# Context attention in a two-layer decoder: probabilities first in the transpose queue, position angles and rope steps moved

## The reference, cut to what matters

```
q = rms_norm((x @ Wq.T).reshape(b, 128, 16, 128), q_norm_w)
kv_in = concatenate([context, x], axis=1)                 # 128 + 128 tokens
k = rms_norm((kv_in @ Wk.T).reshape(b, 256, 4, 128), k_norm_w)
v = (kv_in @ Wv.T).reshape(b, 256, 4, 128)
q, k = rope(q, positions), rope(k, all positions)         # x*cos + rotate_half(x)*sin
probs = softmax(q @ k.T / sqrt(128))                      # 16 query heads, 4 key/value heads
x = layernorm(x + (probs @ v) @ Wo.T)
```

## Time and profile before

| what | value |
|---|---|
| median of 3 runs | 3082.08 us (3080.01 to 3082.26) |
| profiled execution, its own time | 3079.49 us |
| its span, first to last instruction | 3077.7 us |
| context attention in it | some 465 to 1373 us |
| busy share of the whole span | PE 87%, DVE 64%, ACT 52%, POOL 43% |
| mean granted TensorE clock | 0.953 of full speed |

### The profile page before, as it was taken

How to read it: one execution, slowest core, us unless ns; L and a number is a source line. 1 busy time by engine, 2 the same in 40 slices (tenths; PEclk the granted TensorE clock), 3 DMA queues, 4 the chain that set the end, 5 groups by cost and what they waited for, 6 DMA issues and landing times. The chain is left out here.

```text
span 3077.7 us, 47741 instructions
## 1 busy us (share of the span) xinstructions
PE 2672.8 (87%) x16117; PEld 1504.0 (49%) x16380; DVE 1956.4 (64%) x3457; ACT 1604.5 (52%) x3757; POOL 1331.9 (43%) x1334
## 2 busy tenths in 40 slices
PE   6788895688888888857995899998989999999998
PEld 4676662344443444423443666665654444444443
DVE  5788986677777777747855788887563223332325
ACT  7999964555555555537434776776532212222111
POOL 4888977866656565603333311111142212222121
PEclk8999997899999999989997899999989999999999
DMA  4111105443334333433003000000012011111101
GB/s 159 41 53 46 44 27 144 98 79 69 76 75 78 72 76 75 77 89 116 1 1 110 22 22 14 14 18 19 15 67 77 31 63 63 60 64 34 63 30 67
DMA packets 287059, 181.05 MB, mean 59 GB/s; under 512 B 243585, under 2 KB 248065, under 8 KB 284706
## 3 DMA queue, kind: packets, MB, share of 16 engines
q1 hardware_dynamic: 286882, 178.74, 22.2%
...
## 5 line engine op out<-in xcount | busy, mean ns | idle before, releaser
L2065 POOL TENSOR_TENSOR s_state<-s_state,s_ct 128x512 f32<-128x512 f32 x256 | 326.6, 1298 | 81.8 <-DVE s_state L2240 79.4
L779 POOL TENSOR_TENSOR m_aTl<-m_prod,m_aTh 128x512 bf16<-128x512 f32 x88 | 101.7, 1155 | 583.9 <-ACT m_aTh L855 583.9
L2240 DVE TENSOR_TENSOR_SCAN s_state<-s_decay,s_psd 128x512 f32<-128x512 f32 x256 | 301.8, 1209 | 67.9 <-PE s_psd L2385 34.2
L1044 DVE TENSOR_TENSOR m_prod<-m_bank,m_gated 128x512 f32<-128x512 f32 x88 | 60.9, 692 | 437.3 <-ACT m_gated L853 437.3
L853 ACT ACTIVATE m_gated<-m_bank 128x512 f32<-128x512 f32 x88 | 52.5, 597 | 435.7 <-PE m_bank L1166 435.7
L1156 PE MATMUL m_bank<-m_xTl,m_wh 128*128 128x512 bf16 x704 | 267.4, 380 | 3.1 <-ACT m_wh L819 1.0
L1155 PE MATMUL m_bank<-m_xTh,m_wh 128*128 128x512 bf16 x671 | 255.0, 380 | 2.4 <-DVE m_prod L1044 2.4
L1572 ACT ACTIVATE a_prob<-a_pss,a_shift,a_qscale 128x256 f32<-128x256 f32 x256 | 141.0, 560 | 204.9 <-DVE a_shift L1686 204.9
L2385 PE MATMUL s_psd<-ident,s_v 128*128 128x128 f32 x1024 | 165.0, 286 | 42.2 <-DVE s_state L2240 21.2
L1705 DVE SCALAR_TENSOR_TENSOR a_pp<-a_prob,a_rtotal,a_pp 128x256 bf16<-128x256 f32 x256 | 185.1, 783 | 21.7 <-ACT a_pp L1588 21.7
L2141 ACT ACTIVATE s_decay<-s_dt,s_nega 128x508 f32<-128x508 f32 x256 | 181.7, 711 | 19.6 <-DVE s_state L2240 19.5
...
## 6 DMA issues: line engine op xcount, KB each, us to landing
...
```

The costliest lines, as they stand in the source:

```text
L2065: pool.tensor_tensor(h, h, ct[t % 4][:, s * P:(s + 1) * P].unsqueeze(1).broadcast_to([P, KB, P]), ALU.mult).then_inc(weighted, 1)
L2240: dve.tensor_tensor_scan(state[i % RING][:, :], decay[t % 2][:, s, :, :].rearrange("p m t -> p (m t)"), ps_d[i % 2][:, :], 0.0, ALU.mult, ...
```

## The change

Four orders change, and no arithmetic:

- SyncE: in each group the transposes of the probabilities are issued ahead of those of the two chunks; before it was the other way round.
- VectorE: a chunk is cut in two parts. Part 0 is the sum of squares, the cosine product and the small step; part 1 the two sine products. In a turn the first chunk's part 0 stays ahead of the low step, and its part 1 moves behind it. For chunk 6, which has only the subtraction, part 0 is empty, so the subtraction moves behind the low step.
- VectorE's waits: part 0 waits for GpSimd's sum of the chunk two before (`roped`), part 1 for that chunk's low part (`t_low`); before, the whole chunk waited for `t_low`.
- GpSimd: the angles move from group 1, between the low parts of two chunks, to group 0, behind the copy of the sequence.

TensorE's and ScalarE's programs are unchanged. The products with the values stand behind both projections before and after.

```diff
--- before.py
+++ after.py
@@ -1395,11 +1395,11 @@
                 for g in range(4):
                     if g == 0 and not last_x:
                         context(s + 2)
-                    if not last:
-                        turn_chunks(s + 1, g, 1 - p)
                     if start == 0 and g:
                         wl.sync(sp, wlow, first_wo + 2 * g + 1, min(first_wo + 2 * g + 3, nchunks))
                     turn_probs(s, g)
+                    if not last:
+                        turn_chunks(s + 1, g, 1 - p)
 
             sp.dma_start(posi[:, :, :].rearrange("p a s -> p (a s)"), positions).then_inc(loaded, 16)
             sp.dma_start(fq[:, :], freqs).then_inc(loaded, 16)
@@ -1493,7 +1493,6 @@
                     if not last_x:
                         if g == 0:
                             x_copy(s + 2)
-                        if g == 1:
                             angles(s + 2)
                         if g == 2:
                             c_low_part(s + 2, p)
@@ -1646,8 +1645,10 @@
                 dve.wait_ge(angle.sem, angle.at(n))
                 dve.tensor_scalar(ang[:, :, :], ang[:, :, :], -PI, PI, ALU.max, ALU.min).then_inc(sines.sem, 1)
 
-            def chunk(n, c, j):
+            def chunk(n, c, j, part):
                 r = c % 2
+                if c >= 6 and part == 0:
+                    return
                 if c >= 6:
                     dve.wait_ge(v_high.sem, v_high.at(n, c - 5))
                     dve.tensor_tensor(vl[j][:, c - 6, :], ps_p[c % 4][:, :], vh[j][:, c - 6, :], ALU.subtract).then_inc(v_low.sem, 1)
@@ -1661,8 +1662,15 @@
                 src = ps_p[c % 4][:, :].rearrange("p (h d) -> p h d", h=4)
                 m = mul[r][:, :].rearrange("p (h d) -> p h d", h=4)
                 o = rot[r][:, :].rearrange("p (h d) -> p h d", h=4)
+                if part == 1:
+                    if c >= 2 or late(n, 1):
+                        dve.wait_ge(t_low.sem, t_low.at(n, c - 1) if c >= 2 else t_low.at(n - 1, 5 + c))
+                    dve.tensor_tensor(o[:, :, 0:64], src[:, :, 64:128], sinw[:, 0, :].unsqueeze(1).broadcast_to([P, 4, 64]), ALU.mult)
+                    dve.tensor_tensor(o[:, :, 64:128], src[:, :, 0:64], sinw[:, 1, :].unsqueeze(1).broadcast_to([P, 4, 64]),
+                                      ALU.mult).then_inc(rope_mul.sem, 1)
+                    return
                 if c >= 2 or late(n, 1):
-                    dve.wait_ge(t_low.sem, t_low.at(n, c - 1) if c >= 2 else t_low.at(n - 1, 5 + c))
+                    dve.wait_ge(roped.sem, roped.at(n, 2 * c - 2) if c >= 2 else roped.at(n - 1, 2 * c + 10))
                 if c or late(n, 1):
                     dve.wait_ge(summed_e.sem, summed_e.at(n, c) if c else summed_e.at(n - 1))
                 dve.tensor_reduce(ss[:, :], sq[:, :].rearrange("p (h d) -> p h d", h=4), AX.X, ALU.add).then_inc(summed.sem, 1)
@@ -1672,9 +1680,6 @@
                     dve.wait_ge(power.sem, power.at(n, c) if c else power.at(n - 1))
                 dve.tensor_scalar(sse[:, :], ss[:, :], 1.0 / HD if c < QC else 1.0, EPS if c < QC else HD * EPS,
                                   ALU.mult, ALU.add).then_inc(summed_e.sem, 1)
-                dve.tensor_tensor(o[:, :, 0:64], src[:, :, 64:128], sinw[:, 0, :].unsqueeze(1).broadcast_to([P, 4, 64]), ALU.mult)
-                dve.tensor_tensor(o[:, :, 64:128], src[:, :, 0:64], sinw[:, 1, :].unsqueeze(1).broadcast_to([P, 4, 64]),
-                                  ALU.mult).then_inc(rope_mul.sem, 1)
 
             def maxima(s, g, p):
                 dve.wait_ge(scored.sem, scored.at(s, g + 1))
@@ -1719,12 +1724,15 @@
                     if g == 0 and not last_x:
                         x_low_part(s + 2, p)
                     if not last:
-                        chunk(s + 1, 2 * g, 1 - p)
+                        chunk(s + 1, 2 * g, 1 - p, 0)
                     prob_low(s, g)
+                    if not last:
+                        chunk(s + 1, 2 * g, 1 - p, 1)
                     if g == 2 and not last_x:
                         bound(s + 2)
                     if not last:
-                        chunk(s + 1, 2 * g + 1, 1 - p)
+                        for part in range(2):
+                            chunk(s + 1, 2 * g + 1, 1 - p, part)
                     if g:
                         attn_low(s, g - 1)
                     elif start != 0:
@@ -1747,10 +1755,12 @@
             for g in range(4):
                 if g == 2:
                     bound(1)
-                chunk(0, 2 * g, 0)
+                for part in range(2):
+                    chunk(0, 2 * g, 0, part)
                 if g < 2:
                     wl.vector(dve, wlow, 4 * g + 4, 4 * g + 6)
-                chunk(0, 2 * g + 1, 0)
+                for part in range(2):
+                    chunk(0, 2 * g + 1, 0, part)
                 if g < 2:
                     wl.vector(dve, wlow, 4 * g + 6, 4 * g + 8)
             turns(turn, dve)
```

## The result

The changed kernel takes 3055.86 us (median of 4 runs, 3054.76 to 3061.73) where the kernel before, run beside it, takes 3081.05. The ratio is 0.9924, with a 95% interval of 0.9907 to 0.9941: 18 to 29 us faster. The forecast was 3067 us, 15 us faster. So the parts of the sum have to be looked at.

What follows compares the result with a forecast made beforehand. VectorE's chain with ScalarE's exponentials was taken to bound each turn. Thirteen turns gave -13 us, turn 14 -2, turns 0 and 15 nothing: -15, so 3064.5 profiled and 3067 us as median, range 3049 to 3089.

Steps and rivals of the forecast that it cites:

- VectorE's chain: Whole turn: VectorE's loop with ScalarE's exponentials, including stalls behind GpSimd's wide instructions, sets the turn's length, 52.6 us.
- Group 0: VectorE's low step, no longer beside GpSimd's sum, falls from 3.46 to 1.7 us (-1.8); the shift may meet angles (+0.2).
- Group 1: Wait and moved sine products +0.4 us; low step -0.5, chunk 3's small step -0.9, shifts of groups 1 and 2 -0.1 and -0.3.
- Group 3: Chunk 2's late transpose lets the exponentials start only 1.6 us early; chunk 6's subtraction costs 0.6; turn 1.0 us shorter.
- The rival without the hold: Group 3: chunk 2's transpose is in time, exponentials start with the shift; some 2.4 us a turn, 3048 us; chance 0.12.
- the hold: Group 3: ScalarE's high part of chunk 4 waits for chunk 2's transpose, delaying exponentials to 943.2 where the shift allows 941.4.
- The angles' cover: GpSimd, group 0: some 5 us of angles go into idle time, 4.29 us still free after the layer norm's power.
- Turn 14: No angles and no table load there, so the stall at chunk 4 nearly goes: -2 us, between -1 and -3.
- Turns 0, 1 and 15: Turn 0 has weight work: 0, between -2 and +2 us; turn 1 like the others, -1.0; turn 15 has no chunks: 0.
- The eaten gain: TensorE becomes last in group 1, or group 2's shift meets GpSimd's next instruction: 0 to 0.5 us a turn, 3079; chance 0.24.
- the slower rival: Shifts of groups 1 and 2 each wait for a fresh GpSimd instruction: +1.15 us a turn, 3097 us; chance 0.14.
- Signs that missed: Profile after: chunk 3's small step near 0.1 us, and GpSimd without a gap of 4 us in group 0.

Runs made afterwards that it cites:

- the kernel that is this rival: The changed kernel with SyncE's order of before, so only VectorE's and GpSimd's parts of the change: 3051.55 us, ratio 0.9909.
- taking the hold away: The changed kernel with SyncE issuing each group's even-chunk transpose ahead of the probabilities, the odd one still behind: 3049.43 us, ratio 0.9900 to the kernel before.
- the angles alone: The kernel before with only GpSimd's angles moved from group 1 to group 0: 3057.61 us, ratio 0.9931.
- the kernel with the sine products moved in group 0 alone: The kernel before with angles in group 0 and sine products behind the low step in group 0 only, SyncE as before: 3034.67 us, ratio 0.9847.

## Why the prediction was right, and where it was not

The direction and the mechanism of a turn were right. The total came out near by partial luck: the turns with a mechanism gave less than their share (10.0 us for 14), and the first and last turns, taken at next to nothing, gave more (11.4 for 1.0).

**What bounds the turn.** "A turn lasts as long as VectorE's chain": right. VectorE waits for TensorE 0.5 us in all from 635 to 1300 us, and that it is "held until an instruction of GpSimd on wide tiles has ended" is shown by the three kernels that only add waits to GpSimd. That it "works without a pause to the next maxima" was misread: in the kernel before VectorE also waits 2.4 us in group 0 of each turn of the loop for ScalarE's high part of the sequence after next (28.5 us, 12 times) and 1.0 in group 3. That does not touch the sum, since the change leaves the first as it was; it is time that no experiment went after.

**Group 0.** Foretold -1.8 for the low step and +0.2 for the shift; measured -1.79 and +0.12 in the mean. Right. The low step runs beside the power of four columns, 1.18 us, and takes 1.67, 0.42 each, so that power does not hold it. The rule of the Trainium skill weighed there (SBUF — State Buffer, section Who interferes with whom) would have it held; on GpSimd's tiles of 512 columns, and on those of 128, the trace agrees with that rule.

**Group 1.** Foretold: wait and sine products +0.4, low step -0.5, small step -0.9, shifts -0.4. Measured: +0.4, -0.51, -0.68, and -0.22 and -0.33 in the two shifts. The wait ahead of the low step is 0.16 us, not 0.4, since the sum of squares waits 0.16 longer for ScalarE; the net is the same. The exponentials of group 2 start 2.8 us early in the mean, for 3.0.

**Group 3.** Foretold: the exponentials are held and come only 1.6 early; in the mean it is 1.4 (44.2 us behind the first maxima before, 42.8 now). Chunk 6's subtraction +0.6: measured 0.6. The turn: -1.0 foretold, -0.8 measured, 51.9 us for 51.6 to 51.8. Right within 0.2 us.

**The rival without the hold was mis-sized.** "a turn gains 3.4 - 0.6 = 2.8, less what shifts fall badly, some 2.4": the kernel that is this rival gains 1.46 a turn and takes 3051.55 us, for 3048. That the time is so near is luck, by the first and last turns again. Most of the difference is in "the maxima with their shift (1.4)", that is a shift of 0.16 us. That holds only with the hold: without it GpSimd is not late either, and the shift takes 1.04. The shift of group 2 takes 0.69 there, where 0.4 was taken. My own price for taking the hold away, 1.3 to 1.8 us, had the same mistake.

**The angles' cover** was named wrongly: "they go where GpSimd idles, with 4.29 us still free after the layer norm's power". In program order they stand ahead of that power, and the wait that hid them is GpSimd's for the layer norm, 65.5 us in 13 turns before, 10.0 after. The cost, nothing, was right.

**Turn 14**: "I take -2", measured -0.14. Group 0 gains 1.4, but with no angles in the turn there is nothing to move out of group 1, and groups 1, 2 and 3 are 0.3, 0.8 and 0.2 us longer. That is the price of VectorE's part (0.3, 0.4 and 0.6 without SyncE's order), so the term missed what the sine products and the subtraction cost there.

**Turns 0, 1 and 15**: "Turn 0 has weight work on all engines: 0", turn 15 zero, turn 1 like the others. This is the term that was off most: 7.3 us in turns 0 and 1 for 1.0, and 2.6 at the end. Of the 7.3 us, 5.7 are there without SyncE's order (the angles alone give 4.2), and 1.5 come with it. That 1.5 is a difference: in turn 0 the moved call to `turn_chunks` also passed the loads of the output weights, which no longer wait behind transposes, and group 0 of turn 1 falls from 17.1 to 13.1 us; the hold takes 1.6 back in group 3 of turn 0 and 1.1 in group 3 of turn 1. The loads' place by itself is worth 5.0 us on the kernel with the sine products moved in group 0 alone. For turn 15 the step that failed is "I cost this at nothing, since VectorE does not wait for TensorE": in group 0 of that turn VectorE does wait for its scores, 3.6 us before and 1.2 after. Between the kernel without SyncE's order and the changed one, which differ in that order alone, this group falls from 11.4 to 9.2 us. The traces show it; the run times do not separate it. The 1.6 us ahead of turn 0 are not explained; starts of turn 0 between 520.3 and 523.6 us occur among these kernels.

**The eaten gain and the slower rival** did not come. TensorE idles 5.3 us ahead of `turn_x` and runs behind it at clock 0.50, as foretold, but its mean granted clock over turns 2 to 13 is 0.95 before and after, and VectorE's wait for scores is 0.5 us in all. The shifts of groups 1 and 2 take 0.78 and 0.36 us in the mean.

**Signs that missed**: the small step of chunk 3 takes 0.33 us, not 0.1 (0.16 is the time of one that nothing holds), and GpSimd still has a gap of 4.4 us in group 0, which the mistake about the angles' cover explains.
